# Both attention phases: layer norms cut into twelve steps, reciprocals in pieces; mixture: routing moved behind two experts' products

## The reference

```python
x = _layernorm(x + _L0_attn_ref(x, ...))            # 16 heads of 8, softmax          phase a
x = _layernorm(x + _L0_xattn_ref(ctx_1024, x, ...)) # 16 heads of 64, 154+512 keys    phase b
x = _layernorm(x + _L0_ffn_ref(x, ...))             # 16 experts, top 2, shared one   phase c
x = _layernorm(x + _L1_attn_ref(x, ...))            # delta rule, 16 heads            phase d
x = _layernorm(x + _L1_xattn_ref(x, ctx, ctx, ...)) # masked cross attention          phase e
x = _layernorm(x + _L1_ffn_ref(x, ...))             # 8 experts, argmax, gelu         phase f
```

## Time and profile before

| what | us |
|---|---|
| median of 3 runs (lowest, highest) | 1805.13 (1804.35, 1808.02) |
| the profiled execution's own time | 1820.91 |
| its span in the profile | 1819.1 |
| PE busy in the span | 1562.8 (86%) |
| DVE busy | 1175.4 (65%) |
| ACT busy | 911.3 (50%) |
| POOL busy | 659.0 (36%) |

### The profile page before, as it was taken

One profiled execution on the slowest core, in us unless ns is written; L12 is line 12 of the kernel. 1 busy time (PEld: TensorE's weight loads), 2 busy tenths in 40 slices (PEclk: granted clock), 3 DMA queues, 4 the chain that ended last, 5 costly groups with the idle time before them and its releaser, 6 DMA issues.

```text
span 1819.1 us, 41205 instructions
## 1 busy us (share of the span) xinstructions
PE 1562.8 (86%) x17780; PEld 806.6 (44%) x17780; DVE 1175.4 (65%) x2306; ACT 911.3 (50%) x1263; POOL 659.0 (36%) x704
## 2 busy tenths in 40 slices
PE   5888878778999999899987988889998899877995
PEld 1222222223334333433422544667777777664442
DVE  6888784777575657557545567566566766555666
ACT  1676664356775686577574133354454543323220
POOL 1110010145664565466463004556755567000000
PEclk9998897889999999999998989899899999987898
DMA  4000002222222332222220100000000001100000
GB/s 145 1 1 1 1 1 79 68 67 68 72 80 68 83 104 68 68 68 83 68 67 14 61 1 1 14 15 15 3 15 15 15 15 34 49 2 1 6 7 12
DMA packets 32406, 70.61 MB, mean 39 GB/s; under 512 B 5328, under 2 KB 7056, under 8 KB 31968
## 3 DMA queue, kind: packets, MB, share of 16 engines
q1 hardware_dynamic: 32224, 67.98, 12.9%
HBM read 47.45 MB, written 20.51 MB: 37 GB/s over the span
## 4 chain that ended last, share of the span: by engine, by line
PE 62%; DVE 26%; ACT 6%; issue 4%; DMA 1%; POOL 1%; SPq 0%; DVEq 0%; ACTq 0%
PE ps L159 59%; DVE a_MX L369 4%; DVE b_mx L833 2%; DVE st L165 1%; PE ps L219 1%; DVE sq L198 1%; DVE st L191 1%; ACT d_XE L162 1%; DVE d_KV L1542 1%; DVE st L202 1%; DVE b_rd L995 1%; DVE st L180 1%; ACT d_L L162 1%; DVE b_VL L780 1%; POOL b_EL L905 1%
## 5 line engine op out<-in xcount | busy, mean ns | idle before, releaser
L905 POOL TENSOR_TENSOR b_EL<-b_X,b_EH 128x1024 f16<-128x1024 f32 x160 | 340.7, 2130 | 323.6 <-ACT b_EH L162 323.4
L833 DVE TENSOR_REDUCE b_mx<-ps 128x2 f32<-128x666 f32 x256 | 217.1, 848 | 130.1 <-PE ps L159 129.9
L1647 POOL TENSOR_TENSOR d_tmp<-d_G,d_XI 128x31 f32<-128x31 f32 (+15 forms) x248 | 128.6, 519 | 281.8 <-DVE d_G L1578 263.0
L887 ACT ACTIVATE b_X<-ps 128x1024 f32<-128x1024 f32 x160 | 163.6, 1023 | 123.8 <-PE ps L159 121.3
L162 ACT ACTIVATE b_EH<-b_X 128x1024 f16<-128x1024 f32 x160 | 169.1, 1057 | 27.6 <-PE ps L159 16.7
L406 ACT ACTIVATE a_E<-ps 128x1024 f32<-128x1024 f32 x128 | 131.1, 1024 | 102.5 <-PE ps L159 102.3
L159 PE MATMUL ps<-b_M,b_S 128*128 128x512 f16 (+1 forms) x768 | 180.5, 390 | 2.2 <-ACT b_X L887 2.1
L369 DVE TENSOR_REDUCE a_MX<-ps 128x2 f16<-128x1024 f32 x128 | 155.1, 1226 | 39.0 <-PE ps L159 38.8
L1650 POOL TENSOR_TENSOR d_XI<-d_XI,d_tmp 128x31 f32<-128x31 f32 (+15 forms) x248 | 138.8, 560 | 19.4
L159 PE MATMUL ps<-b_Hk,b_Hq 64*128 64x333 f16 x512 | 84.4, 326 | 42.8 <-DVE b_mx L833 37.5
L388 POOL TENSOR_TENSOR a_QS<-a_QS,a_MR 128x512 f16<-128x512 f16 x16 | 18.5, 1156 | 256.8 <-ACT a_MR L162 256.8
(11 more groups left out here) (304 smaller groups left out, 3251.8 us busy)
## 6 DMA issues: line engine op xcount, KB each, us to landing
b_S<-s_xk SPq DMA_DIRECT2D x48, 336.0 KB, 6.3
b_M<-s_xq SPq DMA_DIRECT2D x48, 256.0 KB, 5.0
s_xk<-b_Hk SPq DMA_DIRECT2D x16, 336.0 KB, 2.2
s_xk<-b_Lk SPq DMA_DIRECT2D x16, 336.0 KB, 2.5
s_xq<-b_Hq SPq DMA_DIRECT2D x16, 256.0 KB, 2.0
s_xq<-b_Lq SPq DMA_DIRECT2D x16, 256.0 KB, 2.0
d_XI<-eye SPq DMA_DIRECT2D x8, 512.0 KB, 3.7
f_w<-f_w SPq DMA_DIRECT2D x1, 2048.0 KB, 8.0
```

What stands on the lines that cost most here:

```text
L833: v.e.tensor_reduce(out, PS[:, bk:bk + 2, 0:333], AX, ALU.max).then_inc(sem("b_mx"), 1)
L887: a.e.activation(b_X[k % 2], PS[:, bk:bk + 2, :], ACT.Exp, scale=0.125).then_inc(sem("b_ex"), 1)
L905: last = p.e.tensor_tensor(b_EL[k % 6], b_X[k % 2], b_EH[k % 6], ALU.subtract)
L1647: e.tensor_tensor(tm, a, x, ALU.mult).then_inc(*p.step())
```

## The change

Seven edits:

1. `normalize(fine=True)` gets one more `yield`, before the subtraction, which makes twelve steps of it, and all norms of phases a and b now use it. A norm's DVE instructions stay the same.
2. The turns of `X` after phase a (`turn_*("A", b)`: four PE transposes and one ACT copy per batch) are gone; nothing reads them. DVE's wait on them before its addition in phase b is gone too.
3. The side work is laid out anew: `A_OUT`, `B_KEY` and `B_OUT` are 13, 13 and 25 slots. The first keys' norm takes two groups of phase a in place of one; the keys 2, 3 and 4 follow at slots 29, 42 and 55, and the keys 5 at slot 99, behind batch 0's norm.
4. The reciprocal of 128x512 becomes four of 128x128, two a slot, and the split into two fp16 halves is made in two pieces of 256 columns, one a slot. The selection matmuls start one slot later.
5. Phase c: the gate and up products of the experts 0 and 1 are emitted ahead of the first routing's transposes; ahead of them DVE does only the routing chain.
6. Experts of batch 1 begin (two steps) within the stretch of the last `b_out`, which is now paced over 35 steps.
7. The clearing of `d_XE` goes from DVE, ahead of the routing chain, to POOL.

```diff
@@ normalize @@
             e.tensor_scalar(st[:, k + 1, :], st[:, k, :], 1.0 / D, None, ALU.mult).then_inc(*v.step())
+            if fine:
+                yield
             v.wait_own()
             e.tensor_tensor(out, x, bc(st[:, k + 1, :], D), ALU.subtract).then_inc(*v.step())
@@ a_out_vector @@
             add_vector(v, b, bank["ao", b], "a_add")
+            yield
             v.wait_ge("a_add", b + 1)
-            yield from normalize(v, xb(b), 1e-5, "xr_A")
+            yield from normalize(v, xb(b), 1e-5, "xr_A", fine=True)
+        A_OUT = 13
+        def a_side(lane, out, keys):
             for b in range(NB - 1):
+                yield from out(lane, b)
                 if b == 0:
+                    yield from keys(lane, 1)
+                yield from later(32 - A_OUT - (B_KEY if b == 0 else 0), ())
...
@@ b_out_vector @@
-            e.reciprocal(b_rd, b_den[b % 2]).then_inc(*v.step())
-            yield
-            v.wait_own()
-            e.tensor_copy(b_rp[:, 0, :], b_rd).then_inc(*v.step())
-            v.wait_own()
-            e.tensor_tensor(b_rp[:, 1, :], b_rd, b_rp[:, 0, :], ALU.subtract).then_inc(sem("b_rt"), 1)
-            for _ in range(2):
+            for q in range(4):
+                c = slice(128 * q, 128 * q + 128)
+                e.reciprocal(b_rd[:, c], b_den[b % 2][:, c]).then_inc(*v.step())
+                if q % 2:
+                    yield
+            for q in range(2):
+                c = slice(256 * q, 256 * q + 256)
+                v.wait_own()
+                e.tensor_copy(b_rp[:, 0, c], b_rd[:, c]).then_inc(*v.step())
+                v.wait_own()
+                e.tensor_tensor(b_rp[:, 1, c], b_rd[:, c], b_rp[:, 0, c], ALU.subtract).then_inc(sem("b_rt"), 1)
                 yield
...
-            v.wait_ge("xt_A", b + 1)
             add_vector(v, b, bank["bo", b], "b_add")
             yield
             v.wait_ge("b_add", b + 1)
-            yield from normalize(v, xb(b), 1e-5, "xr_B")
-        B_OUT = 16
+            yield from normalize(v, xb(b), 1e-5, "xr_B", fine=True)
+        B_OUT = 25
+        def b_side(lane, last, keys, out, turn):
+            yield from last(lane, NB - 1)
+            for k in range(2, 5):
+                yield from keys(lane, k)
+            yield from later(6 * 11 + 5 - B_FROM - A_OUT - 3 * B_KEY, ())
             for b in range(NB - 1):
+                yield from out(lane, b)
                 yield from later(3, ())
+                turn(lane, "B", b)
+                if b == 0:
+                    yield from keys(lane, 5)
+                yield from later(44 - B_OUT - 3 - (B_KEY if b == 0 else 0), ())
@@ c_experts_tensor @@
-                if p < 8:
+                if p == 1:
+                    run(begun)
+                for k in (0, 1) if p == 1 else range(p, p + 1 if 1 < p < 8 else p):
                     t.wait_ge("c_ct", b + 1)
...
@@ c_order @@
-            clear(lane)
-            weave((route(lane, 0), 1))
-            weave((tail, 23), (experts(lane, 0), 9))
-            weave((experts(lane, 1), 9))
+            begun = route(lane, 0)
+            next(begun, None)
+            second = experts(lane, 1)
+            weave((tail, B_OUT + 10), (both(experts(lane, 0, begun), part(second, 2)), 11))
+            run(second)
```

More of the change, by code:

```diff
@@ L452, in a_out_tensor @@
             last.then_inc(sem("a_out"), 1)
-            for _ in range(3):
-                yield
+            yield from later(A_OUT - 1, ())
         def a_out_scalar(a, b):
@@ L459, in a_out_scalar @@
             copy(a.e, a_oT[b % 2], PS[:, bank["at", b], :]).then_inc(sem("a_ot"), 1)
-            for _ in range(4):
-                yield
+            yield from later(A_OUT, ())
         def a_out_vector(v, b):
@@ L560, in a_vector @@
                 a_project_vector(v, 0, k)
-            next(keys)
-            side = a_side_vector(v)
+            side = a_side(v, a_out_vector, b_keys_vector)
             for p in range(NG + 2):
@@ L668, in build @@
         B_KEYS_OF = (2, 3, 5, 6)
+        B_KEY = 13
         def b_keys_tensor(t, k, banks=ring):
             kind, i = B_KEYS[k]
-            for _ in range(5):
-                yield
+            yield from later(B_KEY, ())
             bk = banks.take(t, ("bkv", k), 1, "b_kv", k + 1)
@@ L972, in b_out_tensor @@
             e, O = t.e, b_OT[b % 2]
-            for _ in range(3):
+            for _ in range(4):
                 yield
@@ L988, in b_out_tensor @@
             last.then_inc(sem("b_out"), 1)
-            for _ in range(4):
+            for _ in range(12):
                 yield
@@ L1166, in b_tail_scalar @@
         def b_tail_scalar(a):
-            yield from later(B_OUT + 6, ())
+            yield from later(3 + B_OUT + 6, ())
             turn_scalar(a, "B", NB - 1)
@@ L1280, in c_experts @@
             if b and 1 < p < 7:
-                for _ in range(3 if p == 2 else 2):
+                for _ in range(3 if p < 4 else 2):
                     next(rest, None)
@@ L2454, in _ @@
                 return
+            d_clear_gpsimd(p)
             for m in range(NH):
```

120 lines of the change are left out of this document (34 added, 86 removed).

## The result

The changed kernel takes 1821.59 us (median of 6 runs, 1815.6 to 1828.79) against 1804.74 for the kernel before in the same comparison (6 runs, 1801.73 to 1809.02): a ratio of 1.0089, 95% interval 1.0062 to 1.0116. It is slower by 0.9%, 17 us; the forecast was 1777, with a chance of 0.90 for "faster". The profiled execution took 1828.79, its span is 1827.0, the granted clock 0.938 (0.934 before).

The account below looks back on a forecast made before the run. PE, busy 86%, bounds it; time is won only where PE waits on DVE work between maxima reductions or runs at half clock. Terms sum to 28.0: 1820.9 becomes 1792.9, less 15.8 for the median, 1777; range 1762 to 1797.

Parts of the forecast that it names:

- Reciprocals: Phase b: the split reciprocals cost DVE what they cost now, and the selection's later start costs nothing; zero (-2 to +2).
- Start of phase c, gain 3.3: Clearing on POOL and four products laid over the routing chain remove PE's wait for `c_oh`: 3.3 us (1 to 5).
- The waits that I named: Start of phase c: PE's wait for `c_oh` gone, one of about 4.5 us for `c_CT` in its place.
- The first keys' norm, gain 1.0: Phase a: spread over a second group, this norm uses that group's free 2.3 us of DVE; 1.0 us (0 to 2.3).
- Phase a, first batch and keys 1, 3.0: Phase a: spread over 26 slots, this side work costs 10.8 us over plain instead of 13.7; gain 3.0 (6.6 to -0.8).
- second batch, 4.2: Phase a: spread over 12 slots, norm and addition cost 6.0 us instead of 10.2; gain 4.2 (5.9 to 2.5).
- The ten slots: Sign in phase a's second batch: ten slots near 23 us instead of 27.10, clock above 0.9.
- Norms of phase b, 9.8: Phase b, three norms in twelve steps: 3.5, 3.5 and 1.5 us over plain instead of 6.1, 7.3 and 4.9; gain 9.8.
- The picture of a hold: Phase b: POOL's instruction holds DVE's norm steps; small instructions take 0.3 to 1.5 us, PE waits 0.55 per held step.
- Keys 2 to 5, gain 2.5: Phase b: four key norms in separate places cost 5.4 us each, 21.6 over plain instead of 24.1; gain 2.5 (+14 to -12).
- After the output projection, 1.2: Phase c, from the output projection's end to the down product: 14.5 us of DVE work against 15.70; gain 1.2 (-1 to 3).
- The slower rival: Phase b: spread steps meet POOL's instruction at its start and are held 1.0 to 1.3 us each; 1820 us, chance 0.07.

Follow-up runs that it names:

- e10: The changed kernel with the four repairs of e4, e5, e6 and e9 together: 1793.99 us, ratio 0.9924 to the kernel before.
- e15: The kernel before with only phase b's output projection of batches 0 to 2, and what follows it, one slot later: 1826.91 us, ratio 1.0093.
- e6: The changed kernel with phase b's output projection and all behind it in its batch one slot later: 1809.73 us, ratio 0.9979 to the kernel before.
- e9: The changed kernel with DVE's multiplications b_OT in the last batch's output three steps later, in the same steps as PE's selections: 1811.5 us, ratio 1.0026.
- e5: The changed kernel with each selection in the mixture's batches 1 to 3 behind its own expert's products, as before: 1819.6 us, ratio 1.0049.
- e4: The changed kernel with the first keys' norm in five steps in one group of phase a, as before: 1818.24 us, ratio 1.0049.
- e16: The changed kernel with phase a's norms in four steps as before, the eight steps left empty: 1828.8 us, ratio 1.0104 to the kernel before.
- e11: The changed kernel with the norms of batches 0 to 2 behind phase b's output projection in four steps, as before: 1831.52 us, ratio 1.014.
- e12: The changed kernel with the norms of keys 2 to 5 in four steps, each begun where it begins now: 1842.39 us, ratio 1.0206.
- e3: e1 with the clearing on POOL, batch 0's routing behind two experts' products and the last output projection woven with batch 0's experts: 1812.32 us, ratio 1.0006.
- e1: The changed kernel with the mixture's functions and the last batch's output as before, keeping the change in both attentions: 1799.62 us, ratio 0.9948.
- e13: e10 with the last batch's output projection woven with batch 0's nine expert steps alone, without batch 1's experts: 1788.79 us, ratio 0.9885.
- e14: e1 with phase b's output projection one slot later and the first keys' norm in one group: 1791.57 us, ratio 0.9907 to the kernel before.
- e2: The kernel before with only the mixture's functions and the last batch's output as changed: 1826.08 us, ratio 1.0084.

## Why the prediction was wrong, point by point

It failed in sign: 28.0 us of gain were summed, 17 of loss came. 45 us are missing, of which the repairs show 30 together (e10), +- 7; for the other 15 no experiment names a cause. The steps, as the prediction put them:

- *"Reciprocals ... Zero, and so is the selection's start one slot later, as nothing waits behind `b_out` but the turn."* The first of the two large failures: the term was put at nothing. I asked who waits behind the projection, not what it must wait for: in the slot where it lands PE needs the bank of `b_VL`, 1.88 us three times. In all it costs 17 by e15 and 20 by e6 (medians), 14.0 and 8 to 11 by the traces of phase b.
- *Start of phase c, gain 3.3.* The second: 9.1 were lost up to the projection. The waits that I named came as forecast (3.59 for `c_CT`; the selection with two experts' products done begins 0.9 earlier in relation to phase b's end, 12.3 against 11.4). I stopped at the selection's start and didn't follow DVE's order behind it, where the multiplications stand three steps ahead of PE's selections and batch 1's routing behind them. 11 us by e9.
- *Not priced at all:* the first selection of batches 1 to 3 behind the down product. I read the new loop as a step of batch 0's start. 4.2 by e5's trace, 7 by its median, again at the edge. The list of edits ahead of the prediction doesn't have it either: its item 5 speaks of the first routing only, the cut of code beside it shows the loop for every batch.
- *The first keys' norm, gain 1.0.* Wrong in sign: it costs 2.8 by the traces of eighteen kernels and 7 by e4's median. In the changed kernel's trace its stretch is 4.5 longer, with half clock that wasn't there.
- *Phase a, first batch and keys 1, 3.0, and second batch, 4.2.* The ten slots came as said (22.30), but the slots behind them gave part of it back: up to the next batch's output 68.10 against 68.00, and 62.6 against 64.2 for the second. The whole spread in phase a is worth 3 +- 7 (e16) where 8 were summed.
- *Norms of phase b, 9.8.* Right in size: 9.2 +- 8 by e11, 13.1 by its trace, four slots in 13.80. The picture of a hold was half right: held steps reach 2.00 where up to 1.5 was named, and some meet the start of POOL's instruction, but PE's wait behind such a step is 0.51 in the row at 919.15, near the 0.55 of the sum.
- *Keys 2 to 5, gain 2.5.* Right in sign, too small. The 39 slots of keys 2 to 4 take 132.30 (the fifth row above), 39/11 of 34.80 would be 123.4; the 14 of keys 5 take 48.70 where plain they would be 44.3. So four norms cost 8.9 + 4.4 = 13.3 over plain, not 21.6, and the gain on them is 10.8. Batch 3 gave some back (7.0 for both, 4.5 forecast). The price of a coarse norm hangs on its slots: in the new ones it would be 21 us more for the four (e12).
- *After the output projection, 1.2.* Right: 14.2 from its end (1002.54 + 7.41) to the down product at 1024.11, against 15.70.
- *The slower rival* gave 1820, and that it hit the time is chance. It named POOL's hold, and the hold is as it said: 11 spread steps wait for nearly a whole instruction of POOL. But the price of 1.0 to 1.3 a step isn't there, the coarse norms in the same places are slower (e11, e12), and phase b, which it had as the place of the loss, is 10.4 shorter than before.

Phase f is the part that nothing here explains. Its 5.4 us against the kernel before come with the 24 us at half clock (1689.8 to 1713.8). The traces of e3 and e4 have the like (1676 to 1700 and 1679 to 1703, granted clock 0.50 in both), those of e1 and e13 don't (0.94 and 0.95 over the 30 and 35 us there). In the table the eighteen traces fall into three groups with nothing between: 124.4 us for e1, e13 and e14, 129 for the kernel before, e2 and e15, 135 for the other twelve. The three with the old attentions are the middle group; of those with the new ones, the two with the old mixture are in the short group and all with the new mixture but e13 in the long one. The clearing on POOL doesn't decide it (e2 and e13 have it too). So 10 of the 25 us between e1 and the changed kernel go with this clock, though no line of phase f differs. Each kernel was profiled once, and what decides the length wasn't tested; it stays open.

## What to carry to other kernels

When a block moves by a slot, list what the block itself needs there (a bank, a copy), not only who needs the block; a shift of one slot cost 8 to 17 us here. In interleaved programs keep the producer's and the consumer's steps in line on every engine: an instruction that stands ahead of its producer holds up all that is behind it, and that may be the next critical chain. When a loop is rewritten for its first pass, read it once more for the others.

## What the runs showed of the hardware

- A DVE instruction of 128x4 that takes 0.16 us alone takes 1.97 to 2.13 when POOL's 128x1024 `b_EL` (2.13) has just begun. What it costs is what stands behind it: 3.31 us of PE's time in a crowded step (e12), 0.51 or none in a spread one (the changed kernel).
- The price of a coarse norm hangs on its slots: e11's first four slots took 19.5 us where the changed kernel's took 13.8, and in e12 one slot alone took 7.70 (from 430.2) where a plain one takes 3.26.
- Identical code in phase f ran 24 us at half clock in the changed kernel and 10 in the kernel before (1688.0 to 1698.2, clock 0.51), and over eighteen kernels it took 124, 129 or 135 us. A profile of one execution can't price a change of 0.5% here: the profiled execution of the kernel before was 16 us over its median, that of the changed kernel 7.
